# Issuing the softmax normalisation earlier and narrowing the waits of the score matmuls in an eight-stage hybrid block

## The reference, cut to what matters

```
x = x + attn_a(layernorm(x))        # cumulative-sum attention
x = x + layernorm(x) @ sign(W).T    # ffn
x = x + attn_b(layernorm(x))        # causal softmax attention, 16 heads of 64
x = x + layernorm(x) @ sign(W).T    # ffn, the same weights
```

## Time and profile before

| | us |
|---|---|
| median of 2 timed runs (1739.23 and 1762.3) | 1750.77 |
| the profiled execution's own time | 1723.5 |
| span of its slowest core, core 3 | 1722.0 |
| spans of all 8 cores | 1711.9 to 1722.0 |
| PE busy | 1023.5 |
| DVE busy | 835.7 |
| ACT busy | 640.9 |

### The profile page before, as it was taken

The page is one execution under the profiler, slowest core; times in us unless marked ns, Lnnn a source line. Parts: engine busy times, 40 slices in busy tenths (PEclk is TensorE's granted clock), DMA queues, the critical chain, the costliest instruction groups (busy, mean ns, idle before and its releaser), DMA issues.

```text
span 1722.0 us, 16188 instructions; the slowest of 8 cores (1711.9 to 1722.0 us)
## 1 busy us (share of the span) xinstructions
PE 1023.5 (59%) x5088; PEld 429.7 (25%) x5088; DVE 835.7 (49%) x1072; ACT 640.9 (37%) x747; POOL 56.9 (3%) x69
## 2 busy tenths in 40 slices
PE   0354333344214845844887877777777787678368
PEld 0121111111001312311433333333333333233123
DVE  0658888988896455455323232323232222135553
ACT  2344443324320150140364646454545555622300
POOL 1000000000000000001000000000000000010000
PEclk9777667776556967966888888888888887789678
DMA  9003220211010300004002020202020200022024
GB/s 246 0 1 37 37 23 15 37 13 12 0 12 8 29 0 25 25 0 37 1 1 19 1 19 1 19 1 19 1 19 1 19 1 1 1 26 23 0 86 159
DMA packets 73156, 42.03 MB, mean 24 GB/s; under 512 B 67696, under 2 KB 67696, under 8 KB 71024
## 3 DMA queue, kind: packets, MB, share of 16 engines
q0 software_dynamic: 66592, 16.78, 10.9%
q1 hardware_dynamic: 6480, 24.21, 4.5%
HBM read 47.28 MB, written 10.49 MB: 34 GB/s over the span
## 4 chain that ended last, share of the span: by engine, by line
PE 46%; DVE 29%; ACT 12%; issue 5%; DMA 5%; DVEq 1%; POOL 1%; SPq 1%; ACTq 0%; POOLq 0%
PE PC L655 7%; PE PC L724 7%; ACT POOLBF L965 4%; PE POB L900 4%; PE PRB L799 4%; PE PRB L845 4%; PE POB L904 4%; PE PRB L822 3%; DVE LNT L409 3%; DVE POOLBF L404 3%; PE PC L923 3%; PE PD L528 2%; DVE POOLBF L598 2%; DVE POOLBF L573 2%; DVE POOLBF L580 2%
## 5 line engine op out<-in xcount | busy, mean ns | idle before, releaser
L965 ACT ACTIVATE POOLBF<-PC 128x1024 bf16<-128x1024 f32 x128 | 131.0, 1023 | 285.0 <-PE PC L928 173.4
L860 DVE CAST POOLBF<-PRB 128x128 bf16<-128x128 f32 x128 | 37.7, 295 | 190.8 <-PE PRB L851 190.7
L900 PE MATMUL POB<-POOLBF 128*65 128x512 bf16 (+1 forms) x320 | 123.8, 392 | 2.6 <-DVE PF L1024 2.6
L1007 PE MATMUL POB<-PF,ONESRB 1*64 1x512 bf16 x64 | 33.1, 518 | 140.9 <-ACT PF L998 81.5
L904 PE MATMUL POB<-POOLBF 128*65 128x512 bf16 (+1 forms) x320 | 116.2, 379 | 0.0
L265 ACT ACTIVATE LNT<-XT 128x2048 bf16<-128x2048 f32 x16 | 30.6, 1910 | 224.5 <-PE PC L655 153.2
L965 ACT ACTIVATE POOLBF<-PD 128x1024 bf16<-128x1024 f32 x96 | 98.2, 1023 | 15.2 <-ACT POOLBF L965 1.7
L528 PE MATMUL PD<-LNT,WSB 128*128 128x512 bf16 x128 | 39.2, 476 | 95.9 <-ACT POOLBF L536 95.9
L655 PE MATMUL PC<-BIG,WSA 128*128 128x512 bf16 x256 | 59.6, 393 | 45.5 <-DVE BIG L610 40.1
L1014 DVE TENSOR_TENSOR BIG<-PF,POB 64x512 bf16<-64x512 f32 x64 | 43.5, 680 | 87.5 <-PE POB L1007 87.5
L314 PE MATMUL POB<-LNT,ONESB 128*1 128x512 bf16 x128 | 40.2, 471 | 70.2 <-DVE LNT L260 44.9
(11 more groups left out here) (157 smaller groups left out, 2095.3 us busy)
## 6 DMA issues: line engine op xcount, KB each, us to landing
XT<-xT SPq DMA_DIRECT2D x8, 1024.0 KB, 17.9
yT<-XT SPq DMA_DIRECT2D x8, 1024.0 KB, 5.1
BIG<-wts POOLq DMA_DIRECT2D x8, 256.0 KB, 7.0
wsgn<-BIG SPq DMA_DIRECT2D x8, 256.0 KB, 2.2
WSA<-wsgn SPq DMA_DIRECT2D x8, 256.0 KB, 3.6
WSB<-wsgn SPq DMA_DIRECT2D x8, 256.0 KB, 3.8
WSA<-wk POOLq DMA_DIRECT2D x4, 256.0 KB, 5.2
WSA<-wv POOLq DMA_DIRECT2D x4, 256.0 KB, 7.2
```

The source lines that it names most:

```text
L900: t.matmul(PO0[0:65, o:o + N], VSB[:, kt * 130:kt * 130 + 65], ep[:, 0:N], start=(kt == 0), stop=(kt == nkt - 1))
L965: return s.activation(ep[:, 0:1024], ps[:, 0:1024], AF.Exp)
```

## The change

Three edits in emit_attnb:

- a score matmul waits only for the Q evacuation of its step, the K evacuation of its key tile and the constants, in place of all units of the pair;
- a value matmul waits, beside its exponential, for the V evacuation of its own key tile;
- the pending norm is issued right behind the first turn's score matmuls, before the unit, the value matmuls and the exponentials of that turn, in place of behind them.

```
-                        wav = [exp_toks[kt]]
+                        wav = [exp_toks[kt], qt_all[9 + kt]]
...
-                        w = list(qt_all)
+                        w = [qt_all[1 + qs], qt_all[5 + kt // 4],
+                             tok_consts]
...
                         exp_toks.append([ts_, None])
+                      if pending_norm[0] is not None:
+                          norm_done = pending_norm[0]()
+                          pending_norm[0] = None
                       if pending:
                           pending.pop(0)()
...
-                      if pending_norm[0] is not None:
-                          norm_done = pending_norm[0]()
-                          pending_norm[0] = None
                     while avq:
```

## The result

The changed kernel takes 1672.95 us (median of 11 runs, 1668.85 to 1692.9), and the kernel before 1721.34 us (median of 10 runs). The ratio is 0.9716, 95% interval 0.9681 to 0.9751: 2.8% faster, clear of 2%. In some executions of any of these kernels the four cores of one die run at a lower granted clock and take longer; the ratios leave such executions out, the medians of these two lists do not. The two runs of before that stood in the table ahead of the prediction (1739.23 and 1762.3) turned out to be the third slowest and the slowest of the ten. The prediction said 1703 with a range of 1672 to 1727, and a ratio of 0.973. The ratio came true; the time lies 30 us under the forecast, at the range's very edge, and against 1721.34 the forecast of 1703 would have been 1%.

A forecast was written before the change was run, and what follows sets the result against it. PE sets the pace in seven pairs and the norm stops it once every step. 35 us of idle plus 12 us of clock gave 47 us, 1723.5 to 1676.5, scaled to 1703 us; range 1672 to 1727.

The forecast's parts named there:

- the last line of the sum: Whole kernel: 47 us gained, 1723.5 to 1676.5 us, ratio 0.973, then put on the two-run median 1750.77 as 1703 us.
- Norm ahead of a unit: Pairs 0 to 6, steps 2 to 4: next scores 0.7 us earlier at 14 places, 1.8 at 7; 22.5 us together.
- Start of a pair: Pairs 1 to 6 gain nothing, since PE then waits for the next pair's weights; pair 0 gains 0.65 us.
- Last pair: No unit or weights there: first broadcast 3.7 us earlier, the other three steps 2.8 us each; 12.1 us together.
- Idle time in all: PE idle time saved over all pairs: 22.5 + 0.65 + 12.1 = 35 us.
- from 140.9 us to about 115: Sign of being right: PE's idle time before the norm's broadcast group falls by this much.
- The clock: Low clock behind norms costs 57 us at 21 places; 17 us comes back, 5 us lost at pair starts, net 12.
- Most places should still fall: Behind most of the 21 norms with a unit, PE's clock should still drop to 1.2 GHz.
- ACT: Exponentials now start 3.1 us behind the last value matmul; costed at nothing, otherwise up to 0.5 us at 7 V places.
- The extra waits: Value matmuls waiting for their V evacuation cost nothing, since all V tiles of a pair precede its attention.
- The narrower waits of the scores: At a pair's start scores no longer wait for the last V evacuation, 0.65 us; worth nothing in pairs 1 to 6.
- The slower rival: At 21 places low-clock work doubles from 5.4 to 10.8 us: 57 us lost against 35 gained, 1773 us; chance 0.05.

The follow-up runs named there:

- run with early weights: Changed kernel with the weights for the pair after next requested at a pair's start, not behind its flush: 1630.85 us, ratio 0.9485 to the kernel before.
- filled kernels: Useless matmuls put ahead of the norm's broadcasts at 21 places: in the kernel before 1673.83 us, ratio 0.9732; in the changed kernel 1632.77 us, ratio 0.9491.
- run with unit between and copies first: Changed kernel with the unit between scores and broadcasts on PE, and both heads copied on DVE ahead of the unit's evacuation: 1649.25 us, ratio 0.958.

## Why the prediction was right or wrong

*The step that failed* is the last line of the sum, "1723.5 to 1676.5 us, a ratio of 0.973. On the median of 1750.77 that gives 1703 us." The sum on the profiled execution's own time was near: 1676.5 against 1672.95. The factor 1.016 took two runs for the level of the kernel before, of which one, 1762.3, lies 2.5% above the fastest of the ten. Eight more put its median at 1721.34, which the profiled 1723.5 had told already. The range was built on the same scale, and so held 1672.95 by 1 us only. Of the three times of before that were at hand, 1723.5, 1739.23 and 1762.3, the lowest was nearest to the level.

*Norm ahead of a unit*, 0.7 and 1.8 us, 22.5 in all: right. The walk from the scores to the unit came out at 4.40 us as worked out, and the idle time ahead of the broadcasts at these 21 places fell from 86.0 to 60.8 us, by 25.2.

*Start of a pair, nothing in pairs 1 to 6*: right, and the run with early weights shows it. The wait for weights grew to 4.59 us where shown ("4 or 5 us" was said). But the text ahead of the prediction gives a wrong reason for the late request: the slices that it overwrites had been read one pair earlier. The request is late only because the code has it there, so the prediction took for given what 40 us could be won from.

*Last pair*, 12.1 us: right, 72.7 to 60.5 in the stretches shown, 12.2 us.

*Idle time in all*, 35 us: the rows give 55.8 off the broadcasts, 22.5 back on the weights, 4.0 off the scores into PC (6.0 to 2.0) and 3.1 back on those into PD (5.1 to 8.2), 34 us net, and the whole stage 36 (30 if core 7 is taken both times). The filled kernels give 41. The one figure for it that the prediction named, "from 140.9 us to about 115", was wrong by 30 us, because it counts the net gain. The starts of pairs 1 to 7 lose 22.4 us ahead of their broadcasts as well (35.1 to 12.7), and by the prediction's own account what six of them lose had to leave this row and come back ahead of the Q units.

*The clock*, 12 us back of 57: 13 by PE's busy time in the stage on the slowest cores, 19 if core 7 is taken both times, 7 by the filled kernels (46 to 39). So the term has the right sign and size, and is not known better than that. Behind the 21 norms PE worked 116 us at 0.50 on core 3 of the kernel before, half of which, 58 us, is loss (57 predicted), and 91 us on core 7 of the changed one: 12.5 us back, where 17 had been put down. "Most places should still fall" was right: on core 7 one of the 21 no longer does. In single places the stretch was 5.4 us and is 5.6, 3.5 and 5.5. At a pair's start it is 5.2 us for 3.1, half of which, 1.05 us, is loss (0.8 predicted). The rule of the Trainium skill that was weighed, page "TensorE: Matmul & The Clock Gate", section "A second HAM failure mode: psum-queue depth-cycling", says that short idles in close order keep paying. The trace agrees, in that the clock still falls at 20 of the 21 places on core 7. That a shorter idle would then bring nothing back is not what happened.

*ACT*: costed at nothing, "it just fits". Right within 3.1 us, and the first thing to bind as soon as DVE and PE are out of the way (42.6 us in the run with unit between and copies first).

*The extra waits* of the value matmuls cost nothing: right. The narrower waits of the scores were given 0.65 us; they brought 3 us alone and nothing that can be measured beside the norm's move. One of the five V tiles of the flush, the first, is used in the third step already and not in the fourth; nothing hangs on it. *The slower rival*: it wants 10.8 us of work at 0.50 behind a norm, and the longest such stretch at the 21 places of core 7 is 6.4 us.

## What to carry to other kernels

An engine that idles in short runs pays twice where its clock falls behind them. Filling such runs with harmless matmuls shows that second price in one run: here 46 us, beside 86 us of idle time ahead of the broadcasts at the same 21 places. When a wait is shortened, look for the transfer that was issued late without harm: moving it brought 40 us here, beside 49 from the change, and nothing on the kernel before. And put a sum on the time of the execution that it was worked out from; a median of two runs is no scale.

## What the runs showed of the hardware

More work made the kernel faster: 294 matmuls without use took 2.7% off the kernel before, and 231 took 2.3% off the changed one, since the granted clock of a middle pair rose from 0.83 to 0.96, and in the changed one from between 0.82 and 0.87 to 0.93 and 0.95. In the kernel before all 48 middle pairs of the eight cores have nearly the same length, 88.6 to 88.9 us, whether a core waits for weights at their starts or not, and the spans of the cores lie within 10 us. In the changed kernel the same instructions take 79.6 to 86.5 us from one pair to the next on one core, with clocks from 0.87 down to 0.82. And a Q unit that started 1.4 us earlier, while the clock was low, moved the next step by 0.7 us only, because the clock came back at the same moment of the pair.
